# The opening of a two-layer transformer kernel rebuilt: rotation by VectorE in halves, fills from two queues, another order of the first loads

## What is computed

```python
# layer 0: adaLN, rotary attention of 16 heads x 16, GELU feed-forward
g1, g2, s1, s2, sh1, sh2 = split(silu(cond) @ ada_w.T + ada_b, 6)
h = layernorm(x) * (1 + s1) + sh1
q, k, v = h @ qkv_w.T + qkv_b
q, k = q * cos + rotate_half(q) * sin, k * cos + rotate_half(k) * sin
x = x + (softmax(q @ k.T / 4) @ v @ proj_w.T + proj_b) * g1
x = x + (gelu((layernorm(x) * (1 + s2) + sh2) @ fc1_w.T) @ fc2_w.T) * g2
# layer 1: RMS norm, factors from a small network of two products
# (w_t1, w_t2), rotary attention, SwiGLU feed-forward
```

## Time and profile before

| | us |
|---|---|
| median of 3 runs | 757.53 (754.43 to 761.17) |
| profiled execution | 755.99 |
| its span, first to last instruction | 754.2 |
| TensorE busy | 715.7 |
| VectorE busy | 652.9 |
| ScalarE busy | 447.4 |
| GpSimd busy | 288.4 |
| granted TensorE clock, mean | 0.988 |

### The profile page before, as it was taken

One profiled execution on the slowest core, in us unless ns is written; L12 is line 12 of the kernel. 1 busy time (PEld: TensorE's weight loads), 2 busy tenths in 40 slices (PEclk: granted clock), 3 DMA queues, 4 the chain that ended last, 5 costly groups with the idle time before them and its releaser, 6 DMA issues.

```text
span 754.2 us, 13183 instructions
## 1 busy us (share of the span) xinstructions
PE 715.7 (95%) x4576; PEld 441.6 (59%) x4576; DVE 652.9 (87%) x1177; ACT 447.4 (59%) x681; POOL 288.4 (38%) x267
## 2 busy tenths in 40 slices
PE   5979989999999999999999999999999999999697
PEld 3643234466645654575546664668546684767497
DVE  3798999999989998999999999998889898966464
ACT  1216774788568764787568777555555554656242
POOL 0512113542554436622663354412563134323343
PEclk9978999999999999999999999999999999999999
DMA  8445662311322220231322234210331133100001
GB/s 324 127 126 140 190 202 57 99 44 43 99 62 81 66 76 23 82 95 43 85 57 74 68 85 137 75 36 8 99 99 43 37 87 91 28 1 2 1 2 56
DMA packets 32882, 59.42 MB, mean 79 GB/s; under 512 B 7856, under 2 KB 12080, under 8 KB 32560
## 3 DMA queue, kind: packets, MB, share of 16 engines
q1 hardware_dynamic: 32816, 58.58, 26.8%
HBM read 39.42 MB, written 18.87 MB: 77 GB/s over the span
## 4 chain that ended last, share of the span: by engine, by line
PE 65%; DVE 14%; issue 6%; ACT 5%; POOL 2%; DMA 1%; SPq 1%; DVEq 0%; ACTq 0%; POOLq 0%
PE ring L847 17%; PE ps_o L799 11%; PE ps_b L864 11%; PE ring L784 7%; PE ring L769 7%; DVE top L1042 7%; PE ring L741 6%; PE ring L817 4%; PE ring L754 2%; ACT pr L1312 1%; PE ring L723 1%; DVE mlp L1130 1%; ACT mlp L1330 1%; ACT hf L1275 1%; DVE turned L1019 1%
## 5 line engine op out<-in xcount | busy, mean ns | idle before, releaser
L1042 DVE TENSOR_REDUCE top<-ring 128x2 fp32r<-128x1024 f32 x256 | 305.2, 1216 | 14.8 <-PE ring L784 13.4
L1312 ACT ACTIVATE pr<-ring 128x1024 f32<-128x1024 f32 x256 | 251.9, 1024 | 70.5 <-PE ring L769 66.5
L1446 POOL TENSOR_TENSOR act_l<-mlp,act_h 128x256 fp32r<-128x256 f32 x128 | 100.2, 783 | 248.6 <-DVE act_h L1144 248.6
L799 PE MATMUL ps_o<-pr,va 128*17 128x512 f32 x1024 | 132.0, 597 | 0.0
L784 PE MATMUL ring<-kt,qt 48*128 48x512 f32 x512 | 112.3, 460 | 10.3 <-DVE top L1042 5.6
L1326 ACT ACTIVATE mlp<-ring,col 128x256 f32<-128x256 f32 x128 | 60.7, 474 | 92.5 <-PE ring L847 70.7
L769 PE MATMUL ring<-qt,kt 49*128 49x512 f32 x512 | 109.4, 456 | 4.9 <-DVE top L1042 1.4
L784 PEld LDWEIGHTS ring<-kt,qt 48*128 48x128 f32 x512 | 47.9, 187 | 80.3 <-issue 28.2
L769 PEld LDWEIGHTS ring<-qt,kt 49*128 49x128 f32 x512 | 46.3, 184 | 80.8 <-issue 27.8
L847 PE MATMUL ring<-hh,wl 128*128 128x256 f32 x384 | 81.7, 295 | 0.9 <-POOL hl L1439 0.5
L1130 DVE SCALAR_TENSOR_TENSOR mlp<-mlp 128x256 f32<-128x256 f32 x128 | 57.7, 451 | 23.9 <-ACT mlp L1333 23.4
(11 more groups left out here) (83 smaller groups left out, 958.8 us busy)
## 6 DMA issues: line engine op xcount, KB each, us to landing
scratch<-high SPq DMA_DIRECT2D x16, 512.0 KB, 3.8
scratch<-low SPq DMA_DIRECT2D x16, 512.0 KB, 4.2
qt<-scratch SPq DMA_DIRECT2D x64, 128.0 KB, 2.6
kt<-scratch SPq DMA_DIRECT2D x64, 128.0 KB, 2.7
mlp<-in_w_split SPq DMA_DIRECT2D x20, 256.0 KB, 3.1
qt<-scratch SPq DMA_DIRECT2D x64, 64.0 KB, 2.6
kt<-scratch SPq DMA_DIRECT2D x64, 64.0 KB, 2.7
xs<-in_x SPq DMA_DIRECT2D x4, 512.0 KB, 4.3
```

Of the source, the lines that this page charges most:

```text
L799: last = nc.tensor.matmul(ps_o[32 * h:32 * h + HD + 1, :], va[:, u % 2, t, QUAD * g + h, :], pr[:, slot, :], start=(t == 0), stop=(t == T ...
L1042: nc.vector.tensor_reduce(top[:, n % 2, 0:4 * T].rearrange("p (e c) -> p e c", e=2)[:, :, c], pair[:, :, :], AX_X, ALU.max, negate=True).t ...
L1312: nc.scalar.activation(pr[:, at % NP:at % NP + 2, :], pair[:, :, :], ACT.Exp, scale=SCALE).then_inc(free, 1)
L1446: nc.gpsimd.tensor_tensor(act_l[:, at % 2, :], src, act_h[:, at % 2, :].bitcast(F32), ALU.subtract).then_inc(act_l_in, 1)
```

## The change

In the prologue VectorE no longer fills kt; GpSimd does it (`ones`) as the first thing of the next block. x of sequence 0 comes in two halves on two semaphores, and col, eye, wf and trig are issued from the next block. The norm's epsilon is added by VectorE (an operation more in layer 0, merged into one that was there in layer 1), and GpSimd's addition goes, in all 17 norms.

The first rotation is VectorE's alone but for the high parts: per half (the two `qk` products of the pair) two products, one sum, one low part, each of 128x512, with the high part on ScalarE between. VectorE also applies the factors to half of the first hf (k = 1). The spills of high and low parts have a semaphore each. A fill's eight transfers are told apart by size: the four that read the high part alone are issued when the high part has landed, the four that read both when the low part has, and for quads 0 and 1 the latter are issued by ScalarE.

From unit 1 on the lists are the same pieces in slightly other orders. The diff, cut to its core:

```diff
@@ prologue
-            sp.dma_start(xs[:, 0], x_v[0]).then_inc(x_in[0], 16)
+            sp.dma_start(xs[:, 0, 0:2], x_v[0][:, 0:2]).then_inc(x_in[0], 16)
+            sp.dma_start(xs[:, 0, 2:4], x_v[0][:, 2:4]).then_inc(x_rest_in, 16)
             sp.dma_start(ada[:, :, 0:2 * C], ada_v[:, :, 0:2 * C]).then_inc(s_ada[0], 16)
-            sp.dma_start(col[:, :], cols).then_inc(s_small[1], 16)
-            sp.dma_start(eye[:, :], ident).then_inc(s_small[2], 16)
-            sp.dma_start(wf[:, 0:PROJ[0]], w_f32[:, 0:PROJ[0]]).then_inc(s_wf[0], 16)
...
-            nc.vector.memset(kt[:, :, :, :].bitcast(F32), 1.0).then_inc(fill, 1)
@@ gpsimd
+                def ones():
+                    nc.gpsimd.memset(kt[:, :, :, :].bitcast(F32), 1.0).then_inc(ones_in, 1)
                 def root(u, n):
...
-                    step(nc.gpsimd.tensor_scalar(rstd[:, a:b], mv[:, a:b, 1], EPS[layer], None, ALU.add))
-                    nc.gpsimd.tensor_tensor(rstd[:, a:b], rstd[:, a:b], minus_half[:, a:b], ALU.pow
+                    nc.gpsimd.tensor_tensor(rstd[:, a:b], mv[:, a:b, 1], minus_half[:, a:b], ALU.pow
@@ vector, norm_var
+                    settled()
+                    if layer == 0:
+                        nc.vector.tensor_scalar(mv[:, a:b, 1], mv[:, a:b, 1], EPS[0], None, ALU.add).then_inc(var_in, 1)
@@ vector, new pieces of unit 0
+                def modulated(u, n, k):
...
+                    nc.vector.tensor_scalar(hf[:, k, :], bank[:, :], mod[:, j, factor:factor + 1],
+                                            mod[:, j, term:term + 1], ALU.mult, ALU.add).then_inc(free, 1)
+                def first_turn(half):
+                    if half == 0:
+                        ve.wait_ge(s_trig, 16)
+                    ve.wait_ge(*emptied("qk", 0, half))
+                    step(nc.vector.tensor_tensor(turned[:, half, :], raw[:, half, :], trig[:, 0, :], ALU.mult))
+                    step(nc.vector.tensor_tensor(sines[:, half, :], raw[:, half, :], trig[:, 1, :], ALU.mult))
+                def first_rotate(half):
+                    settled()
+                    op, to = ((ALU.subtract, first_turned), (ALU.add, turned_in))[half]
+                    nc.vector.tensor_tensor(turned[:, half, :], turned[:, half, :], sines[:, 1 - half, :], op
+                                            ).then_inc(to, 1)
+                def first_low(half):
+                    ve.wait_ge(*((first_high_in, 1), (high_in, 1))[half])
+                    ins = nc.vector.tensor_tensor(low[:, half, :], turned[:, half, :], high[:, half, :].bitcast(F32),
+                                                  ALU.subtract)
...
@@ scalar
+                def first_lift(half):
+                    ac.wait_ge(*((first_turned, 1), (turned_in, 1))[half])
+                    nc.scalar.activation(high[:, half, :], turned[:, half, :], ACT.Copy
+                                         ).then_inc((first_high_in, high_in)[half], 1)
+                def fill(n):
+                    ac.wait_ge(*low_landed(0, n // 2))
+                    ac.wait_ge(ones_in, 1)
+                    for part in fill_parts(n, 2):
+                        nc.scalar.dma_start(*part).then_inc(slot_in[n], 16)
@@ sync, fill
-                    sp.wait_ge(*spill_landed(u, g // 2))
+                    sp.wait_ge(*high_landed(u, g // 2))
...
+                    for part in fill_parts(n, 1):
+                        sp.dma_start(*part).then_inc(slot_in[n % NSLOT], 16)
+                    if n >= 2:
+                        sp.wait_ge(*low_landed(u, g // 2))
+                        for part in fill_parts(n, 2):
+                            sp.dma_start(*part).then_inc(slot_in[n % NSLOT], 16)
```

More of the change, by code:

```diff
@@ L103, in rope_pieces @@
 def rope_pieces(u, pair):
+    if u == 0 and pair == 0:
+        return [("dve", "first_turn", 0), ("dve", "first_turn", 1), ("dve", "first_rotate", 0), ("act", "first_high", 0),
+                ("dve", "first_rotate", 1), ("act", "first_high", 1), ("dve", "first_low", 0), ("dve", "first_low", 1),
+                ("sp", "spill", u, pair)]
     return [("dve", "cosine", u, pair), ("pool", "sine", u, pair), ("dve", "rotate", u, pair),
@@ L109, in first_pieces @@
 def first_pieces():
[L111 to L114, removed]
+    pieces = [("sp", "load", "col"), ("sp", "load", "eye"), ("sp", "load", "wf"), ("sp", "load", "trig"),
+              ("pool", "ones"), ("act", "silu"), ("dve", "silu"), ("pe", "mod_0", 0),
+              ("dve", "norm_stats", 0, 0), ("dve", "norm_var", 0, 0), ("pool", "root", 0, 0), ("dve", "norm_rows", 0, 0),
+              ("dve", "mod_0", 0), ("pe", "norm_turn", 0, 0), ("act", "modulated", 0, 0, 0), ("dve", "modulated", 0, 0, 1)]
     for pair in range(2):
@@ L117, in first_pieces @@
             pieces += [("pe", "qk", 0, c), ("act", "take", 0, c)]
-        pieces += rope_pieces(0, pair) + [("sp", "fill", pair)]
+        pieces += rope_pieces(0, pair) + [("sp", "fill", pair), ("act", "fill", pair)]
         if pair == 0:
@@ L121, in first_pieces @@
                 pieces += [("pe", "v", 0, t), ("dve", "take_v", 0, t)]
-    pieces += [("pe", "mod_0", 1), ("dve", "mod_0", 1)]
+    pieces += [("pe", "mod_0", 1), ("dve", "mod_0", 1), ("dve", "half_gate")]
     for b in range(B):
@@ L217 @@
 ORDER = {
[L218 to L226, removed]
@@ new lines @@
+        ("pool", "ones"): (0,),
+        ("act", "silu"): (4,),
+        ("dve", "silu"): (9,),
+        ("pe", "mod_0"): (7, 55),
+        ("dve", "norm_stats"): (3, 291, 48, 581, 250, 845, 519, 1137, 779, 1403, 1092, 1652, 1343, 1892, 1542, 2068,
+        2075),
+        ("dve", "norm_var"): (13, 293, 68, 607, 267, 846, 550, 1142, 819, 1423, 1101, 1663, 1368, 1900, 1600, 2069,
+        2089),
+        ("pool", "root"): (47, 284, 78, 660, 208, 894, 552, 1075, 855, 1421, 1047, 1649, 1337, 1893, 1551, 2011,
@@ new lines @@
+        ("dve", "half_gate"): (28,),
+        ("dve", "widen"): (11, 14, 15, 22),
+        ("pe", "gates"): (49, 66, 67, 81),
+        ("dve", "gates"): (53, 69, 70, 83),
+        ("pe", "net_1"): (10,),
+        ("dve", "net_1"): (35,),
+        ("act", "net_gate"): (31,),
+        ("dve", "net_gate"): (45,),
+        ("pe", "net_2"): (76, 77, 80, 86, 87, 88, 93, 100),
+        ("dve", "net_2"): (102,),
+        ("sp", "load_w"): (16, 57, 132, 133, 135, 212, 213, 214, 216, 287, 296, 375, 1342, 1373, 1427, 1457, 1458,
@@ L550, in build @@
         high_in, low_in = sem("high_in"), sem("low_in")
-        spilled = [sem(f"spilled{i}") for i in range(2)]
+        high_spilled = [sem(f"high{i}_spilled") for i in range(2)]
+        low_spilled = [sem(f"low{i}_spilled") for i in range(2)]
+        ones_in, first_turned, first_high_in = sem("ones_in"), sem("first_turned"), sem("first_high_in")
         slot_in = [sem(f"slot{i}_in") for i in range(NSLOT)]
@@ L1007, in take_v @@
                                             ALU.add).then_inc(free, 1)
+                def modulated(u, n, k):
+                    j, layer = UNITS[u]
+                    factor, term = (mod_at(layer, n, what, k) for what in range(2))
+                    bank, full, free, before = place("h1", u, k)
+                    ve.wait_ge(*emptied("mod_0", 0))
+                    ve.wait_ge(full, before + 1)
+                    nc.vector.tensor_scalar(hf[:, k, :], bank[:, :], mod[:, j, factor:factor + 1],
[15 more added lines that the diff above has]
+                                                  ALU.subtract)
+                    if half:
+                        ins.then_inc(low_in, 1)
                 def cosine(u, pair):
                     at = 2 * u + pair
-                    if at == 0:
-                        ve.wait_ge(s_trig, 16)
                     for half in range(2):
                         ve.wait_ge(*emptied("qk", u, 2 * pair + half))
-                    if at:
-                        ve.wait_ge(low_in, at)
+                    ve.wait_ge(low_in, at)
                     nc.vector.tensor_tensor(turned[:, :, :], raw[:, :, :],
```

223 lines of the change are left out of this document (119 added, 104 removed), and 147 rows, old and new, of the table ORDER.

## The result

| | before | after |
|---|---|---|
| median, us | 756.49 | 774.11 |
| lowest to highest | 754.43 to 761.17 | 772.84 to 775.04 |
| ratio, 95% interval | | 1.0223 [1.0171, 1.0274] |
| profiled execution | 755.99 | 774.34 |
| its span | 754.2 | 772.2 |

The kernel before ran beside it on the same chip (756.49). The change costs 17.6 us, 2.2%, and the interval lies wholly above 1. I had predicted 753.3 (748 to 760).

What follows compares the result with a forecast made beforehand. TensorE was taken as the bound, busy 715.7 of 754.2 us. Peaks 2.6, splits 1.3 and the tail's norm 0.3 made 4.2 us won, from the median of 757.53 to 753.3, range 748 to 760.

Steps and rivals of the forecast that it cites:

- the opening up to the spill: Timeline from kt's fill to the low spill: mod_0 at 7.7, transposes 14.7, qk 17.5, low parts through 29.1, spill 29.2.
- Rival C: Opening: gain lost because kt's fill holds up silu (2.5 us) or slot 0 comes at 41 and beyond; 756 to 757, chance 0.20.
- the first step: First fill, quad 0: slot 0 full at 39 (37.2 to 41), so peaks start 4.7 us earlier and end 2.6 earlier.
- the second step: TensorE's stretch from 120 to 700 us: a new order can lose or win some microseconds of the 8.1 idle.
- the sign of it: Forecast is wrong if PE's idle time in 120 to 700 us differs from 8.1 by more than the opening's shift.
- the third step: Clock around quad 0's peaks, 43 to 61 us: falls again behind the first peaks (753.3) or holds, 2.8 us more (750.5).
- rival D: Quad 0: clock falls already within the peaks, last peaks 3.7 us later, 2.1 us lost overall; 759.6, chance 0.13.
- Case B: Clock holds from 43 to 61 us, 2.8 us on top of the 4.2; 7.0 us won, 750.5, chance 0.24.
- the splits: Two splits of weights, 0.64 us each, leave the VectorE-bound stretch behind quad 0's peaks for the opening's idle time; 1.3 us won.

Runs made afterwards that it cites:

- e1: The changed kernel with t2's 1 MB load issued behind the load of x of sequence 1, not between first spill and first fill; 765.41 us.
- e2: The changed kernel with wf1's 1 MB load issued behind fill 4, not right ahead of fill 8; 767.72 us.
- e3: The changed kernel with both loads moved, t2 behind x of sequence 1 and wf1 behind fill 4; 758.42 us, ratio 1.0036 to before.
- e6: e3 with TensorE's net_1 put back behind the first product of v, its readers and weight loads later too; 756.79 us, ratio 1.0006 to before.
- e9: e3 with the loads of x2 and wf1 issued together behind fill 5; 758.02 us, ratio 1.0008 to before.
- e10: e6 with the loads of x2 and wf1 issued together behind fill 5; 754.83 us, ratio 0.9968 to before.
- e8: e3 with unread products added on TensorE ahead of and among quad 0's peaks; 761.5 us, ratio 1.0065 to before, its profiled run 750.82.
- e5: The kernel before with only t2's 1 MB load moved behind the first spill, ahead of the first fill; 764.99 us, ratio 1.0107 to before.
- e11: e10 with the unread TensorE products of e8 added; 755.82 us, ratio 0.998 to before.

## Why the prediction was wrong

*Right: the opening up to the spill.* kt's fill 2.66 us (3), `mod_0` at 7.72 (7.7), transposes at 14.54 (14.7), `qk` at 17.55 (17.5), low parts through at 28.1 (29.1), low spill issued 28.15 (29.2). Rival C's first half is half right: `silu`'s operation on VectorE lasted 0.81 us, to 6.20, just as GpSimd's fill ended at 6.17. But with a fill of 2.66 us that was over before `mod_0`'s weights landed, and it cost nothing.

*Wrong, the first step: "slot 0 is full between 37.2 and 41; I take 39".* It was full at 45.8. I had seen t2 there and priced its megabyte with the stage's mean of 219 GB/s and at worst half that. The runs show something else: with t2 ahead the small transfers of the fill take 5.3 to 12.4 us each instead of 2.8, those issued by ScalarE included, t2 itself takes 12.2, and what is moved in 37 to 40 us is 162 GB/s at a busy share of 1.04. The Trainium skill, "DMA: Bandwidth & Descriptors" (Queues, rings and completion order), says that each DMA engine takes one queue's descriptors in ring order. The traces fit that: in the opening and at fill 8 the slot was full only after the load ahead had landed. But 28.75 + 12.2 = 41 would only have been the earliest time for slot 0. The fills' own transfers took 4.8 us more behind it, and at fill 8 2.0 (188.1 to 190.2). So 41, my upper bound, was in fact the lower one, and nothing stood above it. Rival C named this place and gave it 756 to 757, since I bounded the slot at 41 "and beyond" without a price for beyond. Taken alone it is worth 8.7 us (e1).

*Wrong, the second step: what I didn't look at.* "From unit 1 on the lists are the same pieces in slightly other orders", and "a new order there can lose or win some microseconds of the 8.1 idle". One of these pieces was wf1, moved from 93.66 to 177.34, straight ahead of a fill. 6.4 us (e2). I had named the sign of it: PE's idle time in 120 to 700 differing from 8.1 by more than the opening's shift; it is 15.5.

*Wrong, the third step: the clock as two cases, a dip behind the peaks or none.* Once the loads are away, the clock falls among quad 0's peaks, as in my rival D (e3, e6, e9, e10), which had 0.13. That e3's 758.4 is near D's 759.6 is luck: D had quad 0's last peaks 3.7 us late, and in e3 they are 0.6 early; e3 loses its 5.2 between quads 3 and 5, of which D said nothing. Case B fits e8's one profile better: its terms up to quad 2 are 2.6, 1.3 and 2.8, together 6.7, and the profile is 6.5 ahead there.

*The gains: there, and gone again.* Between quads 0 and 2, where the splits were to give 1.3 us, e3 wins 2.0 and e10 1.8. No run isolates the splits, and e5, which has none of the change, wins 1.6 back there from its late start, so this fits the term but doesn't show it. What e10 wins at quad 3, 4.5 us, it gives back 4.0 of by quad 5: 1.7 from quad 3 to 4, 2.3 from 4 to 5. In the second of these stretches TensorE is busy 19.55 of 21.98 us at clock 0.92; before it is busy 17.93 of 19.67 at 1.00:

```profile
111.28:130.95 19.67, 17.93 (x98) 8.61 (x94) 18.80 (x37) 8.47 (x10) 6.66 (x6) 1.00 0.22 64
```

```profile
108.44:130.42 21.98, 19.55 (x102) 9.84 (x98) 20.10 (x39) 9.59 (x12) 7.84 (x6) 0.92 0.42 122
```

e8's profile speaks for the clock (0.7 us lost from quad 3 to 5 at 1.00, with the pieces of e3), but no experiment separates the two in e10. What makes the clock hold in one run and fall in the next stays open; that the unread products hold it isn't shown (e8: one of eight; e11: lower end 751.3, median no better than e10's).

## What to carry to other kernels

When an order of transfers is rewritten, list every large load with the small transfer issued next behind it that an engine will wait for, over the whole kernel and not only in the stage that the change is about; a load of 1 MB issued right ahead of such a transfer cost 8.7 and 6.4 us here, where its bytes at the opening's mean rate would have made 4.8. Look as well for what reads the load itself: in e5 that alone cost 8 us. Here the loads did least harm where no transfer that an engine waits for followed for 6 to 7 us (wf1 before, x2 and wf1 in e10). And where a stretch's clock decides some microseconds, take several runs: one profile shows one of its outcomes.

## What wasn't expected of the hardware

- Issuing itself took longer with the megabyte there: SyncE needs 1.44 us to issue t2 and 1.57 us for the two transfers behind it (1.44 and 1.48 in e2), against 0.81 for these two in e1. Why isn't shown.
- The DMA engines' busy share says little of what is moved: 1.04 at 162 GB/s in 37 to 40 us (after), 1.04 at 352 GB/s in 40 to 43 (e3).
- In after TensorE is busy 3.00 of every 3 us from 46 to 61 by its records, and the granted clock is 0.50 (1.2 GHz) in all of these windows, behind the 8.8 idle us; it is 1.00 again only from 70 on (0.57 in 67 to 70). The Trainium skill, "TensorE: Matmul & The Clock Gate" (The HAM clock gate), says that sustained activity releases the gate; measured by the records' busy time, that didn't happen in this stretch.
- GpSimd fills 128x3072 in 2.66 us, VectorE in 2.62: for a fill the two are alike.
